# Gating and head-mix bias moved from VectorE to ScalarE and GpSimd in a fused attention-and-FFN layer

## The reference, cut to what matters

```python
xn = layernorm(x)
# s: four heads of 128, mixed by a 512x512 matrix
local_out  = softmax(q_l k_l^T * scale) v_l           # full attention over 1024 rows
sparse_out = softmax(where(score >= kth largest, score, -1e9)) v_s   # k = 102 of 1024
mem_out, pred_out = small heads, row by row
s = concat([local_out, sparse_out, mem_out, pred_out]) @ warboss_w + warboss_b
# g: an FFN of width 2048
g = silu(relu(xn @ w1 + b1) @ w2 + b2)
return x + s * g
```

## Time and profile before

| | |
|---|---|
| time, median of 3 runs | 2740.56 us (2732.62 to 2744.57) |
| span of the profiled execution, first to last instruction | 2731.8 us (8.8 us below the median; 0.8 us below the fastest run) |
| stage 2, from the first `sc` copy | 548.3 us to the end |
| mean granted clock of TensorE | 0.991 |
| busy: PE, DVE, ACT, POOL | 2646.1, 2415.3, 1704.5, 1801.4 us |

### The profile page before, as it was taken

How to read it: one execution, slowest core, us unless ns; L and a number is a source line. 1 busy time by engine, 2 the same in 40 slices (tenths; PEclk the granted TensorE clock), 3 DMA queues, 4 the chain that set the end, 5 groups by cost and what they waited for, 6 DMA issues and landing times.

```text
span 2731.8 us, 43928 instructions
## 1 busy us (share of the span) xinstructions
PE 2646.1 (97%) x13537; PEld 2221.8 (81%) x13537; DVE 2415.3 (88%) x5223; ACT 1704.5 (62%) x3038; POOL 1801.4 (66%) x1562
## 2 busy tenths in 40 slices
PE   6999999899999999999999999999999999999997
PEld 5888888677888888888888888887888888888886
DVE  6555555499999999999999999999999999999996
ACT  4565655565666666666666666666666666666664
POOL 2000000176788778877887788778877887788787
PEclk9999999999999999999999999999999999999998
DMA  6333344421222212221222122212221222122212
GB/s 210 136 142 126 128 146 144 142 79 47 62 79 77 68 60 84 72 70 55 85 75 72 55 86 70 70 55 86 71 70 58 86 70 70 59 89 70 70 58 89
DMA packets 224924, 235.24 MB, mean 86 GB/s; under 512 B 13843, under 2 KB 151763, under 8 KB 222677
## 3 DMA queue, kind: packets, MB, share of 16 engines
q1 hardware_dynamic: 224724, 232.75, 26.9%
HBM read 165.59 MB, written 67.11 MB: 85 GB/s over the span
## 4 chain that ended last, share of the span: by engine, by line
PE 66%; DVE 10%; issue 2%; POOL 1%; ACT 1%; DMA 0%; DVEq 0%; POOLq 0%; ACTq 0%; SPq 0%
PE hid L65 7%; PE hid L67 7%; PE hid L66 7%; PE acc L67 7%; PE acc L66 7%; PE acc L65 7%; PE o L1263 6%; PE scores L1249 4%; DVE larger L1152 3%; DVE top_l L1137 2%; PE o L67 2%; PE o L65 2%; PE o L1266 2%; PE o L66 2%; PE scores L67 2%; PE scores L66 2%
## 5 line engine op out<-in xcount | busy, mean ns | idle before, releaser
L975 POOL TENSOR_TENSOR w_lo<-w,w_hi 128x512 fp32r<-128x512 f32 x514 | 685.1, 1354 | 3.9 <-ACT w_hi L823 3.9
L1137 DVE MAX8 top_l<-larger 128x8 f32<-128x512 f32 x832 | 572.8, 688 | 13.2
L1152 DVE MATCH_REPLACE8 larger<-top_l,larger 128x512 f32<-128x512 f32 x768 | 518.5, 675 | 0.0
L975 POOL TENSOR_TENSOR h_lo<-h,h_hi 128x512 fp32r<-128x512 f32 x256 | 341.0, 1332 | 253.2 <-ACT h_hi L860 251.6
L65 PE MATMUL hid<-xnT_hi,w_hi 128*128 128x512 f32 x1024 | 417.4, 408 | 29.5 <-DVE xnT_lo L1177 27.5
L975 POOL TENSOR_TENSOR tl_lo<-tl,tl_hi 128x512 fp32r<-128x512 f32 x65 | 84.2, 1296 | 529.0 <-ACT tl_hi L823 528.4
L67 PE MATMUL hid<-xnT_hi,w_lo 128*128 128x512 f32 x1024 | 402.0, 393 | 0.0
L66 PE MATMUL hid<-xnT_lo,w_hi 128*128 128x512 f32 x1024 | 401.8, 392 | 0.0
L65 PE MATMUL acc<-w_hi,h_hi 128*128 128x512 f32 x1024 | 399.1, 390 | 1.8 <-POOL w_lo L975 1.8
L67 PE MATMUL acc<-w_hi,h_lo 128*128 128x512 f32 x1024 | 400.0, 391 | 0.0
L66 PE MATMUL acc<-w_lo,h_hi 128*128 128x512 f32 x1024 | 399.7, 390 | 0.0
(11 more groups left out here) (164 smaller groups left out, 6182.3 us busy)
## 6 DMA issues: line engine op xcount, KB each, us to landing
w<-in_L_ffn_w SPq DMA_DIRECT2D x260, 256.0 KB, 2.7
xin<-in_L_attn_x SPq DMA_DIRECT2D x18, 1024.0 KB, 6.3
units<-kv_scratch SPq DMA_DIRECT2D x72, 256.0 KB, 3.2
units<-xnT_scratch SPq DMA_DIRECT2D x68, 256.0 KB, 3.2
tl<-tile_scratch SPq DMA_DIRECT2D x65, 256.0 KB, 2.7
xnT_scratch<-xnT SPq DMA_DIRECT2D x16, 1024.0 KB, 8.1
kv_scratch<-kv_out SPq DMA_DIRECT2D x32, 512.0 KB, 2.7
tile_scratch<-tiles_out SPq DMA_DIRECT2D x16, 1024.0 KB, 4.3
```

The source lines that it names most:

```text
L975: return nc.gpsimd.tensor_tensor(out_, value, hi_.bitcast(F32), ALU.subtract).then_inc(ready, 1)
L1137: l_step = count(nc.vector.max(top_l[:, own], larger[:, :]))
L1152: l_step = count(nc.vector.match_replace(larger[:, :], top_l[:, own], larger[:, :], LOWEST))
```

## The change

VectorE's part of `gates` and the whole of `mix` are taken off it. For each tile of a half ScalarE still writes tanh into `gate`, and then copies the FFN output out of `acc` into a new tensor `ffn_out` of one tile. GpSimd, which now has `gates` between `head_out` and `transposed` of slots 0 and 4, multiplies `gate` by `ffn_out` and then adds `ffn_out`, two instructions, the second of which waits for the first. As there is one `ffn_out`, ScalarE's copy of a tile waits for `gate_ready` of the tile before. For the mix, ScalarE copies `o` with scale 0.5 into `mixed` at the place where it had waited for `mix_done` anyway, and GpSimd adds `half_bias` between the third chunk and `tl_lo`. `at`, which had a place for each head, has one place now, and ScalarE waits for GpSimd's `at_l` before it writes there.

```diff
@@ scalar
                 def head_out(i, head):
                     act.wait_ge(pv_done, i + 1)
-                    nc.scalar.activation(at[:, head, :, :], o[:, 0:2 * P].rearrange("p (i n) -> p i n", n=P), ACT.Copy)
+                    if not known_first(i, 1):
+                        act.wait_ge(at_l, i)
+                    nc.scalar.activation(at[:, :, :], o[:, 0:2 * P].rearrange("p (i n) -> p i n", n=P), ACT.Copy)
...
-                        nc.scalar.activation(gate[:, t, :], acc[:, t, :], ACT.Tanh, scale=0.5).then_inc(tanh_ready, 1)
+                        nc.scalar.activation(gate[:, t, :], acc[:, t, :], ACT.Tanh, scale=0.5)
+                        if t > 0:
+                            act.wait_ge(gate_ready, HTILES * h + t)
+                        elif not known_first(h, 1):
+                            act.wait_ge(gate_ready, HTILES * h)
+                        nc.scalar.activation(ffn_out[:, :], acc[:, t, :], ACT.Copy).then_inc(tanh_ready, 1)
+
+                def mixed_of(m, t):
+                    act.wait_ge(mix_done, m + 1)
+                    if not known_first(m, HTILES):
+                        act.wait_ge(prod_ready, m - HTILES + 1)
+                    nc.scalar.activation(mixed[:, t, :], o[:, :], ACT.Copy, scale=0.5).then_inc(mix_read, 1)
...
-                            act.wait_ge(mix_done, m)
+                            mixed_of(m - 1, (T - 1) % HTILES)
                         split_tl(m + 1, (T + 1) % 2)
@@ gpsimd
+                def gates(h):
+                    for t in range(HTILES):
+                        pool.wait_ge(tanh_ready, HTILES * h + t + 1)
+                        nc.gpsimd.tensor_tensor(gate[:, t, :], gate[:, t, :], ffn_out[:, :], ALU.mult)\
+                            .then_inc(gated, 1)
+                        pool.wait_ge(gated, HTILES * h + t + 1)
+                        nc.gpsimd.tensor_tensor(gate[:, t, :], gate[:, t, :], ffn_out[:, :], ALU.add)\
+                            .then_inc(gate_ready, 1)
+
+                def bias_of_mixed(m, t):
+                    pool.wait_ge(mix_read, m + 1)
+                    nc.gpsimd.tensor_tensor(mixed[:, t, :], mixed[:, t, :], half_bias[:, :], ALU.add)\
+                        .then_inc(mix_ready, 1)
...
                             head_out(2 * m - 2, 0)
+                        if T % HTILES == 0 and some:
+                            gates(2 * b + T // HTILES - 1)
                         if some:
                             transposed(2 * m - 1)
...
+                        if some:
+                            bias_of_mixed(m - 1, (T - 1) % HTILES)
                         split_tl(m + 1, (T + 1) % 2)
...
+                gates(2 * B - 1)
                 residual(last + HTILES, HTILES)
                 transposed(2 * B * TILES - 1)
                 residual(last + HTILES + 1, HTILES + 1)
                 head_out(2 * B * TILES - 1, 1)
+                bias_of_mixed(B * TILES - 1, HTILES - 1)
                 for T in range(HTILES + 2, TILES):
@@ vector
-                        nc.vector.scalar_tensor_tensor(out=gate[:, t, :], in0=gate[:, t, :], scalar=1.0,
-                                                       in1=acc[:, t, :], op0=ALU.add, op1=ALU.mult)\
-                            .then_inc(gate_ready, 1)
...
-                    nc.vector.scalar_tensor_tensor(out=mixed[:, t, :], in0=o[:, :], scalar=0.5, in1=half_bias[:, :],
-                                                   op0=ALU.mult, op1=ALU.add).then_inc(mix_ready, 1)
```

More of the change, by code:

```diff
@@ L649, in stage2 @@
         pT_s = sb("pT_s", [P, TILES, 2, P], F32R)
-        at = sb("at", [P, 2, 2, P], F32)
+        at = sb("at", [P, 2, P], F32)
         at_hi = sb("at_hi", [P, 2, P], F32R)
@@ L656, in stage2 @@
         xin = sb("xin", [P, D], F32)
+        ffn_out = sb("ffn_out", [P, D], F32)
         scores = ctx.enter_context(nc.psum_tensor("scores", [P, S], F32))
@@ L701, in stage2 @@
         mix_ready = sem("mix_ready")
+        mix_read = sem("mix_read")
+        gated = sem("gated")
         at_left = sem("at_left")
@@ L970, in _ @@
                 head_out(2 * B * TILES - 1, 1)
+                mixed_of(B * TILES - 1, HTILES - 1)
             @block.gpsimd
@@ L1003, in head_out @@
                     pool.wait_ge(at_h, i + 1)
-                    lo(at[:, head, 0, :], at[:, head, 0, :], at_hi[:, head, :], at_left)
+                    lo(at[:, 0, :], at[:, 0, :], at_hi[:, head, :], at_left)
                     pool.wait_ge(at_left, i + 1)
-                    nc.gpsimd.tensor_tensor(at_lo[:, head, :], at[:, head, 0, :], at[:, head, 1, :], ALU.add)\
+                    nc.gpsimd.tensor_tensor(at_lo[:, head, :], at[:, 0, :], at[:, 1, :], ALU.add)\
                         .then_inc(at_l, 1)
+                def gates(h):
[10 more added lines that the diff above has]
+                        .then_inc(mix_ready, 1)
                 def residual(m, T):
@@ L1083, in apply_threshold @@
                     nc.vector.reciprocal(inv[:, 1:2], sums[:, 1:2]).then_inc(invs_ready, 1)
-                def gates(h):
-                    for t in range(HTILES):
-                        dve.wait_ge(tanh_ready, HTILES * h + t + 1)
-                        nc.vector.scalar_tensor_tensor(out=gate[:, t, :], in0=gate[:, t, :], scalar=1.0,
-                                                       in1=acc[:, t, :], op0=ALU.add, op1=ALU.mult)\
-                            .then_inc(gate_ready, 1)
-                def mix(m, t):
-                    dve.wait_ge(mix_done, m + 1)
-                    if not known_first(m, HTILES):
-                        dve.wait_ge(prod_ready, m - HTILES + 1)
-                    nc.vector.scalar_tensor_tensor(out=mixed[:, t, :], in0=o[:, :], scalar=0.5, in1=half_bias[:, :],
-                                                   op0=ALU.mult, op1=ALU.add).then_inc(mix_ready, 1)
                 def full_max(m):
@@ L1111, in full_inverse, with search @@
                     nc.vector.reciprocal(inv[:, 0:1], sums[:, 0:1]).then_inc(invl_ready, 1)
-                def search(m, T, b):
+                def search(m, T):
                     done = [1 + STEPS * T]
@@ L1141, in search @@
                             s_step = count(nc.vector.max(top_s[:, own_s], smaller[:, :]))
-                        if r == R_MIX and not known_first(m, 1):
-                            mix(m - 1, (T - 1) % HTILES)
-                        if r == R_GATES:
-                            gates_of_half(m, T, b)
                         if r == r_max:
@@ L1166, in search @@
                     assert done[0] == 1 + STEPS * (T + 1)
-                def gates_of_half(m, T, b):
-                    if T % HTILES == 0 and not known_first(m, 1):
-                        gates(2 * b + T // HTILES - 1)
                 def split_xn(h):
@@ L1192, in slots @@
                             dve.wait_ge(step, 1)
-                        search(m, T, b)
+                        search(m, T)
                         if T % HTILES == HTILES - 1:
@@ L1200, in _ @@
                 apply_threshold(B * TILES - 1, TILES - 1)
-                gates(2 * B - 1)
-                mix(B * TILES - 1, HTILES - 1)
             @block.tensor
```

## The result

The changed kernel takes 2935.94 us (median of 4 runs, 2931.69 to 2944.53) against 2740.74 us for the kernel before in the same comparison: a ratio of 1.072, 95% interval 1.0689 to 1.0749. It is 7.2% slower. The profiled execution took 2937.41 us, of which its span is 2935.6, so 1.8 us lie around a span.

The account below looks back on a forecast made before the run. The prediction took TensorE as the bound, VectorE a hair behind. Stall 146, clock 27, end 18 and VectorE 5 gave +196 on a 2731.8 us span, 2928, plus 8.8 around it: 2937 us, 7.2% slower; range 2900 to 2970.

Parts of the forecast that it names:

- The stall: Before `scores` in slots T = 0 and 4, TensorE waits for copies queued behind the gating: 15 half boundaries, 146 us.
- The clock: Behind each of 15 new TensorE pauses, 1.8 us of work is lost to a lower granted clock: 27 us.
- The end: At the program's end, gating rounds, later mix, bias ahead of residual 62 and late `xin` of 63: +18 us.
- VectorE and its neighbours: At half boundaries, removing one `mix` relieves VectorE, but GpSimd's added instruction lengthens `xnT_lo`: +5 us net.
- a lag of VectorE is worked off before T = 3: VectorE's lag from T = 0 and 4 is gone before T = 3, so only one `mixed`, 0.67 us, counts.
- Batch 0: In batch 0, where VectorE is late from the start, relieving it gains about 2 us.
- What lies around the span: Median run time lies 8.8 us (0.3%) above the profiled span; this is added to the forecast span.
- GpSimd slowed in the gating: Rival 1: GpSimd's gating instructions take 1.73 us each, adding 39 + 3 us, 2979 us in all; 10%.
- TensorE held only at `f2`: Rival 2: TensorE waits only at `f2(C)` for the fourth gate, 7.0 us each, 105 in all, 2896 us; 7%.
- Gating hidden: Rival 3: VectorE is the bound and the gating rounds fit in slack; 2721 us, 0.7% faster; 3%.

Follow-up runs that it names:

- two_outs: Changed kernel with a second place for the FFN output (tiles 1 and 3 in a free part of `h32`): 2871.28 us, ratio 1.049 to the kernel before.
- copies_first: Changed kernel with the copies of the transposed probabilities ahead of the gating in slots 0 and 4, on ScalarE and GpSimd: 2947.09 us, ratio 1.074.
- filled_pause: Changed kernel with 38 extra matmuls, result unused, on TensorE in each of the 15 pauses before `scores`: 2906.98 us, ratio 1.062.
- mix_only: Kernel before with only the head mix moved to ScalarE's copy and GpSimd's bias, the gating left on VectorE: 2796.18 us, ratio 1.021.
- spread_mix_back: Changed kernel with `acc` copied at once, tanh, product and sum done one tile a slot, and the mix back on VectorE: 2798.36 us, ratio 1.022.
- memsets: Kernel before with three unneeded GpSimd memsets a slot, which read nothing, ahead of `tl_lo`: 2812.59 us, ratio 1.028.

## Why the prediction was right, and where it wasn't

- **The stall**, 146 us forecast, 139.9 measured. The mechanism is the one that was named, place, count and releaser. In T = 4 a round took 3.31 us and not 3.49, because from multiply to add it took 1.34 to 1.35 us and not 1.46, and the add itself 1.27 and not 1.30. Three rounds too long by 0.18 are 0.5 us at a boundary; 9.65 against 8.98 is 0.67, and the other 0.16 is the counting: the profile counts the wait from the end of the last matmul (1871.01 + 0.39), the forecast from where the next would have started, 0.23 us behind its start. In T = 0 the rounds were as short, and the forecast of 9.8 us came out (9.97) because GpSimd also reached the gating 0.7 us later against TensorE than in the kernel before, behind the 3.44 us of `w_lo`. The prediction had no such term; that the sum is within 6 us is in part luck. `two_outs` shows that the one tile is what makes the rounds, `copies_first` that TensorE pays them at either place.
- **The clock**, 27 us forecast. TensorE's busy time rose by 2.2 us at each boundary, 33 for 15, and by 38.6 over the whole span; `filled_pause` gave back 29 us. The term was too small because the window that I read, 680 to 685, has 0.64 in the mean; behind the new pauses the whole 5 us are at 0.50. After the pause of 4.80 us nine matmuls came slowly (679.64 to 683.62), after those of 9 us twelve (5.17 us).
- **The end**, +18 forecast, 50.0 - 30.3 = 19.7 measured. The rounds, the bias ahead of residual 62 and the late `xin` (2.12 us of wait) all show.
- **VectorE and its neighbours**, +5 forecast. By its own terms it is 7 x 0.4 + 8 x 0.9 - 2 = 8; the steps from there to 7 and to 5 have no reason given. It was right for the sum and wrong as a picture. Before T = 4 the four `xnT_lo` took 5.54 us and not 4.47, one more long one, as worked out. But I had let only `xnT_lo` be hit. VectorE's busy time per batch was to fall by 10 us and rose by 1.1, since `smaller` went from 720 to 1539 ns, `xnT_lo` from 1270 to 1462. In the combined kernel that costs little: VectorE stands 7.4 us at each boundary for TensorE and gets into step there. In `mix_only`, where no stall gives it that time, the same instruction costs 57 us. So "the mix is nearly free" held only beside a larger loss, and the step that failed, unseen in the sum, was that a lag of VectorE is worked off before T = 3 whatever GpSimd does.
- **Batch 0** was to gain 2 us. Its first five slots went from 167.25 to 181.65 us, 14.4, of which a boundary explains 12.2; the other 2 are a loss (the last section shows its place).
- **What lies around the span** was taken as 8.8 us, the distance to the median; it is 1.8. The span came out at 2935.6, 8 us above the forecast 2928; what is added to it was 7 us too much. The two errors cancel, so the hit of the total (2937 against 2935.9) is closer than the working deserves.
- **The rivals.** GpSimd slowed in the gating: no, 1.26 to 1.29 us there. TensorE held only at `f2`: that is `copies_first`, and it costs as much, since a round stands in front of each of the four tiles and the clock falls for all four; my 105 us for it left both out. Gating hidden: `spread_mix_back` hides it from TensorE's `scores`, and loses 62 us, some 50 in the slots and 12 at the end.

With terms as measured the sum is 139.9 + 33 + 19.7 = 193 of 203.8 us. Of the other 11, 2 are in batch 0. The two boundary slots of a batch grew by 12.2 + 11.8 = 24.0 us, of which two stalls are 18.7 (139.9 / 15 each) and the clock 4.5: 0.8 us a batch is left, 6 us in seven batches, and the four `xnT_lo` before T = 4, 1.07 us longer, are enough for it. The last 3 us I can't put down to a row.

## What to carry to other kernels

Idle time of an engine is not free room if another engine's slow pair of operands was lying in it: look at what the neighbour does in that gap before an instruction is put on the idle engine, and count the instructions that are moved back, not the one that is added. When work leaves an engine through a buffer of one tile, the chain of copy, product and sum becomes a round trip per tile, and it is paid at whichever wait comes first behind it; and a pause of TensorE cost its length here and then a stretch at the lower clock, 2.2 us behind 9.

## What the runs showed of the hardware that was not expected

GpSimd and VectorE hold each other up both ways, for VectorE mostly in steps rather than in proportion: `smaller` is 0.68 us or about 1.78 in all but one of its 64 executions in each of these kernels. `larger` is mostly 0.69 or 1.44 but also 0.9 and 1.66, and a GpSimd `h_lo` goes from 1.29 over 1.75 up to 2.3. The Trainium skill ("SBUF — State Buffer", Who interferes with whom) says that a VectorE instruction with two inputs from SBUF contends with a GpSimd instruction that reads SBUF and not with one that only writes. The rows agree with the first half; no row here tests the second by itself. That memsets cost 75 us all the same is no contradiction, since they moved the reading instructions behind them.

A single VectorE instruction can be held for far longer than the one GpSimd instruction beside it. In the changed kernel `ranked`, 57 numbers wide, took 7.68 us in batch 0, where it takes 0.54 to 1.37 us in the kernel before (timeline of VectorE, then of GpSimd):

```profile
610.14 7.68 DVE L1183 TENSOR_TENSOR ranked<-top_l,top_s 128x57 f32<-128x57 f32 x1
```

```profile
609.80 1.32 POOL L995 TENSOR_TENSOR h_lo<-h,h_hi 128x512 fp32r<-128x512 f32 x1
...
614.78 2.55 POOL L995 TENSOR_TENSOR w_lo<-w,w_hi 128x512 fp32r<-128x512 f32 x2
```

GpSimd ran six instructions without a gap from 609.80 to 617.33, at its undisturbed 1.3 us each, and VectorE came through only when the row of back-to-back instructions ended. TensorE then stood 4.49 us for the probabilities behind it and resumed at half the clock (0.50 from 620 to 625). It happened twice in this trace (6.52 us in the other case, at 2294.58), and in `mix_only` `ranked` took 3.5 us twice; which of the two engines gets through in such a row, and why VectorE alone lost here, where elsewhere both did, stays open.
